# The end of an FFN kernel: the last quarter of the last tile as two pieces of 128 columns

## The chip, the cores and the metric

The kernel runs on one core of a Trainium2 chip. The metric is the device time of one execution in microseconds (us); lower is better. The kernel before was executed three times: 496.27, 496.76 and 497.31 us, median 496.76 us. One more execution was profiled; its own time and span stand in the table below.

## The reference

A grouped 1-D convolution with a conditioning term is followed by a dense layer with a low-rank correction, and all of it is added to the input. Cut to what matters:

```python
# x: (64, 64, 1024); 4 groups of 16 channels; 9 taps
y = conv1d(x, weight, groups=4) + (cond @ c_weight.T)[:, :, None] + fside[None, :, None]
base  = y @ kernel + bias                      # kernel: 1024 x 1024
A_eff = einsum('bn,nri->bri', gate, lora_A)    # 8 batches, rank 32
B_eff = einsum('bn,nor->bor', gate, lora_B)
delta = (y @ A_eff.T) @ B_eff.T + (y @ A_shared.T) @ B_shared.T
out = x + base + delta
```

## The kernel before

The 64 x 64 rows of x are worked in 8 batches (`b`) of 4 groups (`g`). A tile is one batch and one group: 128 rows of 1024 columns. There are 32 tiles in all, and the very last is `b = 7, g = 3`.

For a tile, TensorE runs the convolution, and then the dense product. Each operand of the dense product is split into a high and a low part of type fp32r (`y_hi`, `y_lo`, `w_hi`, `w_lo`), and three products are summed in PSUM: hi by hi, hi by lo, lo by hi. The contraction of 1024 is cut into `KC` = 8 chunks of 128 (`k`). So one column range of a tile is 8 x 3 = 24 matmuls, each with its own 128 x 128 stationary operand (a piece of `y`), and one more matmul (98 rows: low-rank part and bias, `b_cur` and `ax_st`) that closes the sum. All matmuls of the dense product that come before the end move 512 columns of `w` each (L921), and the matmul that closes them is L926. The low-rank product of `y` with A (L934) moves 256 columns past a 64-column stationary operand.

PSUM has two accumulators `main[0]` and `main[1]`, 1024 columns each, that is two banks of 512 each. Tiles alternate between them. VectorE (DVE) adds a finished tile to `res`, which holds x, and counts `main_free` up; the queue of SyncE (SP) waits for `main_free` and sends the tile out of `res`.

The last tile is not done like the others. Its parts, in order:

1. columns 0 to 511 in `main[1]`, 24 matmuls of 512 columns and L926;
2. the third quarter, columns 512 to 767, in the other bank of `main[1]`: `quarter(2, k)`, 24 matmuls of 256 columns (L909), and `quarter_rank(2)` (L912);
3. the last quarter, columns 768 to 1023, in `main[0]`, in the same form. Before it TensorE waits until DVE has emptied `main[0]` of the tile before.

Each of the parts counts `tile_done` up; DVE adds it (L789 for the first, L794 for the quarters), and SP stores it (L317):

```python
for n, part in enumerate((slice(0, 512), slice(512, 768), slice(768, 1024))):
    sp.wait_ge(main_free, NB * G + n)
    sp.dma_start(out_t[...], res[:, G - 1, part])
for g in range(G):
    sp.wait_ge(stored[g], 16 * (NB + 2 * (g == G - 1)))
```

The program ends when SP has seen every store's completion. Every engine's stream is in program order, written by hand; no scheduler moves anything. The functions that the change touches:

Of the kernel before, what the change touches and what calls it, by code (L numbers as in the profile page):

```python
# [7 lines left out]
ALU = mybir.AluOpType  # L8
# [3 lines left out]
P = 128  # L12
NS, C, L = 64, 64, 1024
D = 1024
G, CG, TAPS = 4, 16, 9
CD = 128
NL, R = 16, 32
NB = 8
# [5 lines left out]
KC = 8  # L24
R8, RQ = 8, R // 8
STACK = 3 * R
ROWS = STACK + 2
# [17 lines left out]


NP = MB // 2
FT = 6
SUM, EVEN, ODD = range(3)


def adaln_ffn(nc, x, x_rows, x_first, small, conv_w, kern, bias, lora_a, lora_b, shared, out):
# [9 lines left out]
    with ctx:  # L62
        def sb(name, shape, dt=F32):
            return ctx.enter_context(nc.sbuf_tensor(name, shape, dt))

        def ps(name, shape):
            return ctx.enter_context(nc.psum_tensor(name, shape, F32))

        def sem(name):
            return ctx.enter_context(nc.semaphore(name))  # L70

        def early(*specs):

            with ExitStack() as own:
                return [own.enter_context(nc.sbuf_tensor(*s)) for s in specs]
# [12 lines left out]
        res = sb("res", [P, G, D])  # L88
        la, = early(("la", [P, RQ, L], F32))
        be_hi, = early(("be_hi", [P, RQ, 512], F32R))  # L90
        xd_hi, xd_lo = sb("xd_hi", [P, 2, NP, SB], F32R), sb("xd_lo", [P, 2, NP, SB], F32R)
        ax_st, ax_sum = sb("ax_st", [P, 2 * P], F32R), sb("ax_sum", [R, 2 * P])
# [6 lines left out]
        x_tr = sb("x_tr", [P, MB + 1, SB, G])  # L99
        x_hi, x_lo = sb("x_hi", [P, 2, 2, NP + 1, SB], F32R), sb("x_lo", [P, 2, 2, NP + 1, SB], F32R)  # L100
        t_hi, t_lo = sb("t_hi", [P, G, WIN, CG], F32R), sb("t_lo", [P, G, WIN, CG], F32R)
# [5 lines left out]
        b_cur = sb("b_cur", [P, D], F32R)  # L107
        ctx_all = sb("ctx_all", [P, G, NS])
        ident, gmix = early(("ident", [P, P], F32), ("gmix", [P, NB, R8], F32))
        xd = sb("xd", [P, NP, SB])  # L110
        y_hi, y_lo = (y_hi0, y_hi1), (y_lo0, y_lo1)

        main = [ps(f"main{i}", [P, D]) for i in range(2)]
# [29 lines left out]
        tile_done, main_free = sem("tile_done"), sem("main_free")  # L143
        res_in = [sem(f"res_in{g}") for g in range(G)]
        stored = [sem(f"stored{g}") for g in range(G)]
# [12 lines left out]

        def x_raw(g, i0=0, i1=NP + 1):
            return x_tr[:, 2 * i0:2 * i1, :, g].rearrange("p (i e) n -> p e i n", e=2)  # L160

        def x_block(e, i0, g):
            return x_tr[:, 2 * i0 + e:2 * i0 + e + 2 * NP - 1:2, :, g]

        def x_half(half):
            return ((0, XSPLIT // 2), (XSPLIT // 2, NP + 1))[half]

# [12 lines left out]

            return b_cur[0:ROWS, :].rearrange("p (oh o8 ol) -> p o8 oh ol", oh=2, o8=R8)[:, 4 * n:4 * n + 4]

        def last_part(q):
            return (main[1][:, 512:768], main[0][:, 0:256])[q - 2]

        def small_part(i):
            return sm[:, SMALL[i]:SMALL[i + 1]]
# [4 lines left out]
        def f_bank(part):  # L192
            return (conv[0], conv[1], spare)[part][:, :]
# [18 lines left out]
        def _(sp):  # L212
# [99 lines left out]
            begin(NB - 1)  # L312
            turns(NB - 1, more_x=False, more_res=False)

            for n, part in enumerate((slice(0, 512), slice(512, 768), slice(768, 1024))):
                sp.wait_ge(main_free, NB * G + n)
                sp.dma_start(out_t[G - 1, (NB - 1) * SB:NB * SB, :, part], res[:, G - 1, part]).then_inc(stored[G - 1], 16)  # L317
            for g in range(G):
                sp.wait_ge(stored[g], 16 * (NB + 2 * (g == G - 1)))


        @block.gpsimd
# [119 lines left out]
        def _(act):  # L442
# [38 lines left out]
            def x_high(u, h, t):  # L481
# [6 lines left out]
                else:  # L488
                    act.wait_ge(conv_ready, u * FT + (3 * t - 7))
                act.wait_ge(xd_done, u * 4 + (2 * t - 7))  # L490
# [83 lines left out]
        def _(dve):  # L574
# [75 lines left out]
            def y_pair(b, h, t):  # L650
# [3 lines left out]
                term = ctx_all[:, 2 * h + t, bass.ds(b * SB, SB)].unsqueeze(1).broadcast_to([P, NP, SB])  # L654
                dve.wait_ge(conv_ready, u * FT + (at + 1))
                dve.wait_ge(y_turned, u * CT + 2 * t)
                nc.vector.tensor_tensor(y_add[:, 1, :].rearrange("p (m n) -> p m n", n=SB),  # L657
                                        f_bank(SUM).rearrange("p (m n) -> p m n", n=SB), term, ALU.add).then_inc(conv_free, 1)
                for e, part in enumerate((EVEN, ODD)):
                    dve.wait_ge(conv_ready, u * FT + (at + 2 + e))  # L660
                    dve.wait_ge(conv_free, u * FT + (at + 1 + e))
                    nc.vector.tensor_tensor(y_add[:, e, :], f_bank(part), y_add[:, 1, :], ALU.add).then_inc(conv_free, 1)
                for e in range(2):
                    dve.wait_ge(conv_free, u * FT + (at + 2 + e))
                    dve.wait_ge(ylo_done, u * CT + (2 * t + e - 5))
# [116 lines left out]
            with dve.Fori(1, NB - 1) as b:  # L782
# [5 lines left out]
            dve.wait_ge(tile_done, NB * G)  # L788
            nc.vector.tensor_tensor(res[:, G - 1, 0:512], main[1][:, 0:512], res[:, G - 1, 0:512],  # L789
                                    ALU.add).then_inc(main_free, 1)  # L790
            for q in (2, 3):
                part = slice(q * 256, (q + 1) * 256)
                dve.wait_ge(tile_done, NB * G + (q - 1))
                nc.vector.tensor_tensor(res[:, G - 1, part], last_part(q), res[:, G - 1, part], ALU.add).then_inc(main_free, 1)  # L794


        @block.tensor
        def _(pe):
            mm = nc.tensor.matmul
# [46 lines left out]
            def fast(b, h, t):  # L846
# [12 lines left out]
                for part in (SUM, EVEN, ODD):  # L859
                    if not (isinstance(u, int) and u == 2 and t == 0):  # L860
                        pe.wait_ge(conv_free, u * FT + (3 * t - 6 + part))
                    (t_h, t_l), (x_h, x_l) = taps[part], blocks[part]
# [39 lines left out]
                              lb[:, oh, s * 512:(s + 1) * 512], start=True, stop=True)  # L902
                last.then_inc(b_mm, 1)

            def quarter(q, k):

                yh, yl = y_hi[1][:, 1, k, :], y_lo[1][:, 1, k, :]
                for lhs, rhs, first in ((yh, w_hi, True), (yh, w_lo, False), (yl, w_hi, False)):
                    mm(last_part(q), lhs, rhs[:, k, q * 256:(q + 1) * 256], start=k == 0 and first, stop=False)  # L909

            def quarter_rank(q):
                mm(last_part(q), ax_st[0:ROWS, P:2 * P],  # L912
                   b_cur[0:ROWS, :].rearrange("p (oh o8 ol) -> p o8 oh ol", oh=2, o8=R8)[:, 2 * q:2 * q + 2],
                   start=False, stop=True).then_inc(tile_done, 1)

            def dense(h, t, k, halves=(0, 1), products=(0, 1, 2)):
                yh, yl = y_hi[h][:, t, k, :], y_lo[h][:, t, k, :]
                for i in products:
                    lhs, rhs, first = ((yh, w_hi, True), (yh, w_lo, False), (yl, w_hi, False))[i]
                    for n in halves:  # L920
                        mm(main[t][:, n * 512:(n + 1) * 512], lhs, rhs[:, k, n * 512:(n + 1) * 512],  # L921
                           start=k == 0 and first, stop=False)
# [86 lines left out]
            def unit(b, h, y=True, final=False, late=False):  # L1009
                u = b * 2 + h  # L1010
                nb, nh = (b, 1) if h == 0 else (b + 1, 0)
                pe.wait_ge(ylo_done, u * CT - 2)
                pe.wait_ge(main_free, u * 2 - 1)
                for k in range(4):
                    dense(h, 0, k)
                if y and not late:
                    fast(nb, nh, 0)
                for k in range(4, KC):
                    dense(h, 0, k)
                pe.wait_ge(ylo_done, u * CT)  # L1020
                pe.wait_ge(acur_done, b + 1)
                pe.wait_ge(ax_summed, u)
                with_a(h)
                pe.wait_ge(main_free, u * 2)

                def first_rank():
                    pe.wait_ge(axlo_done, u + 1)
                    if not (isinstance(b, int) and b == 0):
                        pe.wait_ge(b_loaded, b * 48)
                    lowrank(0)  # L1030

                if final:
                    for k in range(KC):
                        dense(h, 1, k, (0,))
                        if k == 4:
                            first_rank()
                    lowrank(1, (0,))
                    for k in range(KC):
                        quarter(2, k)
                    quarter_rank(2)  # L1040
                    pe.wait_ge(main_free, NB * G - 1)
                    for k in range(KC):
                        quarter(3, k)
                    quarter_rank(3)
                    return
                for k in range(3):
                    dense(h, 1, k)
                if not late:
                    first_rank()
                if y:  # L1050
                    fast(nb, nh, 0 if late else 1)
                if late:
                    first_rank()
                for k in range(3, 6):
                    dense(h, 1, k)
                if y and late:
                    fast(nb, nh, 1)
                for k in range(6, KC):
                    dense(h, 1, k)
                lowrank(1)  # L1060

            unit(0, 1, late=True)
            with pe.Fori(1, NB - 1) as b:
                unit(b, 0)
                unit(b, 1)
# [44 lines left out]
```

## Time and profile before

| what | value |
|---|---|
| median of 3 runs | 496.76 us |
| profiled execution, its own time | 497.13 us |
| profiled execution, span first to last instruction | 495.3 us |
| TensorE busy | 486.8 us, 98% of the span |
| VectorE busy | 319.3 us, 64% |
| GpSimd busy | 270.6 us, 55% |
| ScalarE busy | 166.9 us, 34% |
| granted TensorE clock, mean | 0.997 |

The profiled execution took 1.8 us more than its span, and 0.37 us more than the median of the runs. TensorE is busy in nearly every slice of the span; the last of the 40 slices of the page (12.4 us each) is the only late one in which it falls off, since the last add and the last store stand there alone.

### The profile page before, as it was taken

The page shows a single profiled execution, that of the slowest core. Times are in us where ns is not written, and L with a number is a line of the kernel's source. Part 1 is how long each engine was busy: PE and PEld are TensorE (multiplying, and loading weights), DVE is VectorE, ACT ScalarE, POOL GpSimd, SP SyncE. Part 2 cuts the span into 40 slices and gives each one's busy share as a digit, 9 for nine tenths or more (in the row PEclk, how much of TensorE's full clock was granted, in tenths as well). Part 3 has the DMA queues.
Part 4 walks back from the last instruction along what each step waited for, and adds up shares of the span by engine and source line. Part 5 has one row for each costly group of instructions (what it writes and reads, how often), then busy time and mean ns, then how long its engine had stood idle before and what let it go on. Part 6 is the DMA issues. An engine that isn't in the chain of part 4 may idle for free.

```text
span 495.3 us, 6738 instructions
## 1 busy us (share of the span) xinstructions
PE 486.8 (98%) x2417; PEld 403.1 (81%) x2417; DVE 319.3 (64%) x368; ACT 166.9 (34%) x205; POOL 270.6 (55%) x153
## 2 busy tenths in 40 slices
PE   6999999999999999999999999999999999999997
PEld 4785988888888888888888888888888888888886
DVE  4757575969667594948937595765939398473402
ACT  4575334333343152323324233431524224331100
POOL 0889865964837275661939247471846519392200
PEclk9899999999999999999999999999999999999999
DMA  8951858543624063431724245240734313241302
GB/s 252 422 233 60 255 122 226 221 134 108 218 53 125 40 232 107 106 95 29 248 72 119 71 152 183 50 129 26 249 90 113 88 36 84 63 123 66 96 32 85
DMA packets 16733, 64.56 MB, mean 130 GB/s; under 512 B 1520, under 2 KB 1968, under 8 KB 15824
## 3 DMA queue, kind: packets, MB, share of 16 engines
q1 hardware_dynamic: 16640, 64.35, 42.2%
q8 instruction: 8, 0.13, 0.1%
q10 hardware_dynamic: 80, 0.04, 0.0%
q14 instruction: 5, 0.04, 0.0%
HBM read 45.10 MB, written 18.87 MB: 129 GB/s over the span
## 4 chain that ended last, share of the span: by engine, by line
PE 97%; DMA 2%; DVE 0%; ACT 0%; SPq 0%; issue 0%
PE main L921 70%; PE rank L934 6%; PE main L926 3%; PE conv L839 3%; PE conv L863 3%; PE conv L864 3%; PE conv L865 3%; DMA x_tr<-in_x_first 2%; PE spare L865 1%; PE spare L864 1%; PE spare L863 1%; PE main L909 1%; PE main L888 1%; PE conv L901 1%; PE spare L876 0%; PE rank L876 0%
## 5 line engine op out<-in xcount | busy, mean ns | idle before, releaser
L921 PE MATMUL main<-w_hi,y_hi 128*128 128x512 f32 x504 | 155.6, 391 | 0.3 <-DVE a_eff L682 0.3
L921 PE MATMUL main<-w_lo,y_hi 128*128 128x512 f32 x504 | 155.1, 390 | 0.0
L921 PE MATMUL main<-w_hi,y_lo 128*128 128x512 f32 x504 | 154.7, 389 | 0.0
L376 POOL TENSOR_TENSOR y_lo<-y_stage,y_hi 128x512 fp32r<-128x512 f32 x56 | 93.2, 1686 | 34.3 <-ACT y_hi L479 34.3
L921 PEld LDWEIGHTS main<-w_lo,y_hi 128*128 128x128 f32 x504 | 94.5, 188 | 20.9 <-POOL w_lo L381 0.8
L921 PEld LDWEIGHTS main<-w_hi,y_lo 128*128 128x128 f32 x504 | 94.6, 188 | 19.9
L921 PEld LDWEIGHTS main<-w_hi,y_hi 128*128 128x128 f32 x504 | 93.4, 188 | 19.6 <-issue 0.7
L356 POOL TENSOR_TENSOR xd_lo<-xd,xd_hi 128x512 fp32r<-128x512 f32 x28 | 40.3, 1441 | 100.4 <-ACT xd_hi L491 100.3
L358 POOL TENSOR_TENSOR x_lo<-x_tr,x_hi 128x1024 fp32r<-128x1024 f32 x28 | 82.3, 2939 | 15.6 <-ACT x_hi L493 15.6
L493 ACT ACTIVATE x_hi<-x_tr 128x1024 fp32r<-128x1024 f32 x28 | 57.6, 2056 | 27.7 <-DVE x_tr L648 27.7
L479 ACT ACTIVATE y_hi<-y_stage 128x512 fp32r<-128x512 f32 x56 | 35.5, 634 | 91.9 <-DVE y_stage L666 91.9
L666 DVE STREAM_TRANSPOSE y_stage<-y_add 128x512 f32<-128x512 f32 x56 | 62.9, 1162 | 0.0
L738 DVE TENSOR_TENSOR ax_sum<-rank,ax_sum 32x256 f32<-32x256 f32 x16 | 6.6, 412 | 76.1 <-ACT ax_sum L504 76.1
L746 DVE TENSOR_TENSOR res<-main,res 128x1024 f32<-128x1024 f32 x31 | 37.5, 1210 | 22.9 <-PE main L926 22.9
L491 ACT ACTIVATE xd_hi<-xd 128x512 fp32r<-128x512 f32 x28 | 17.7, 633 | 90.9 <-DVE xd L644 90.9
L648 DVE TENSOR_TENSOR x_tr<-x_tr 128x512 f32<-128x512 f32 x28 | 44.7, 1597 | 1.0
L644 DVE TENSOR_TENSOR xd<-x_tr 128x512 f32<-128x512 f32 x28 | 40.0, 1428 | 1.2 <-POOL xd_lo L356 1.2
L657 DVE TENSOR_TENSOR y_add<-conv,ctx_all 128x512 f32<-128x512 f32 x28 | 19.2, 686 | 24.2 <-PE conv L865 24.2
L934 PE MATMUL rank<-y_hi,a_cur 128*64 128x256 f32 x128 | 29.9, 277 | 0.0
L934 PE MATMUL rank<-y_lo,a_cur 128*64 128x256 f32 x128 | 29.9, 277 | 0.0
L606 DVE STREAM_TRANSPOSE x_tr<-x_in 128x512 f32<-128x512 f32 (+2 forms) x48 | 29.4, 680 | 0.2
L504 ACT ACTIVATE ax_sum<-rank 32x256 f32<-32x256 f32 x16 | 6.0, 375 | 64.8 <-PE rank L934 64.8
(102 smaller groups left out, 503.3 us busy)
## 6 DMA issues: line engine op xcount, KB each, us to landing
res<-in_x SPq DMA_DIRECT2D x32, 512.0 KB
out<-res SPq DMA_DIRECT2D x31, 512.0 KB
x_in<-in_x_rows SPq DMA_DIRECT2D x6, 2048.0 KB, 12.5
w_raw<-in_L_ffn_kernel SPq DMA_DIRECT2D x4, 1024.0 KB, 16.8
b_cur<-b_scratch SPq DMA_DIRECT2D x21, 128.0 KB, 3.1
x_tr<-in_x_first SPq DMA_DIRECT2D x1, 2064.0 KB, 8.8
la<-in_L_ffn_lora_A SPq DMA_DIRECT2D x4, 512.0 KB, 10.1
lb<-in_L_ffn_lora_B SPq DMA_DIRECT2D x1, 2048.0 KB, 24.8
```

The source lines that it names most:

```text
L356: nc.gpsimd.tensor_tensor(xd_lo[:, t], xd[:, :, :], xd_hi[:, t].bitcast(F32), ALU.subtract).then_inc(xlo_done, 1)
L358: nc.gpsimd.tensor_tensor(x_lo[:, t, :, 0:NP], x_raw(2 * h + t, 0, NP), x_hi[:, t, :, 0:NP].bitcast(F32), ALU.subtract).then_inc(xlo_done, 1)
L376: nc.gpsimd.tensor_tensor(y_parity(y_lo, h, t, e), y_staged(e), y_parity(y_hi, h, t, e).bitcast(F32), ALU.subtract).then_inc(ylo_done, 1)
L479: nc.scalar.activation(y_parity(y_hi, h, t, e), y_staged(e), ACT.Copy).then_inc(yhi_done, 1)
L493: nc.scalar.activation(x_hi[:, t, :, 0:NP], x_raw(2 * h + t, 0, NP), ACT.Copy).then_inc(xhi_done, 1)
L606: nc.vector.transpose(x_tr[:, m0:m1, :, :].rearrange("p m n g -> p m (n g)"), blocks).then_inc(xt_done, 1)
L644: nc.vector.tensor_tensor(xd[:, :, :], x_block(0, 1, g), x_block(1, 0, g), ALU.subtract).then_inc(xd_done, 1)
L648: nc.vector.tensor_tensor(x_block(0, 0, g), x_block(0, 0, g), x_block(1, 0, g), ALU.subtract).then_inc(xd_done, 1)
L666: nc.vector.transpose(y_stage[:, e, :].rearrange("p (a l n c) -> p a n l c", a=2, l=2, n=SB), y_add[:, e, :].rearrange("p (a m n) -> p a n ...
L746: nc.vector.tensor_tensor(res[:, g, :], main[g % 2][:, :], res[:, g, :], ALU.add).then_inc(main_free, 1)
L921: mm(main[t][:, n * 512:(n + 1) * 512], lhs, rhs[:, k, n * 512:(n + 1) * 512], start=k == 0 and first, stop=False)
L934: last = mm(rank[0:2 * R, 0:2 * P], lhs, y[h][:, :, k, :], start=k == 0 and y is y_hi, stop=k == KC - 1 and y is y_lo)
```

## The change

The last quarter of the last tile becomes two pieces of 128 columns, 768 to 895 and 896 to 1023. Each has its own 24 matmuls and its own closing matmul, its own bank of `main[0]`, its own add and its own store. A list `LAST` holds the column bounds of the three pieces that follow the first half. The third quarter, columns 512 to 767, stays as it is.

```diff
+LAST = [512, 768, 896, 1024]
...
-        def last_part(q):
-            return (main[1][:, 512:768], main[0][:, 0:256])[q - 2]
+        def last_part(n):
+            return (main[1][:, 512:768], main[0][:, 0:128], main[0][:, 512:640])[n]
...
-            for n, part in enumerate((slice(0, 512), slice(512, 768), slice(768, 1024))):
+            for n, part in enumerate((slice(0, 512), *(slice(LAST[i], LAST[i + 1]) for i in range(3)))):
                 sp.wait_ge(main_free, NB * G + n)
                 sp.dma_start(out_t[G - 1, (NB - 1) * SB:NB * SB, :, part], res[:, G - 1, part]).then_inc(stored[G - 1], 16)
             for g in range(G):
-                sp.wait_ge(stored[g], 16 * (NB + 2 * (g == G - 1)))
+                sp.wait_ge(stored[g], 16 * (NB + 3 * (g == G - 1)))
...
-            for q in (2, 3):
-                part = slice(q * 256, (q + 1) * 256)
-                dve.wait_ge(tile_done, NB * G + (q - 1))
-                nc.vector.tensor_tensor(res[:, G - 1, part], last_part(q), res[:, G - 1, part], ALU.add).then_inc(main_free, 1)
+            for n in range(3):
+                part = slice(LAST[n], LAST[n + 1])
+                dve.wait_ge(tile_done, NB * G + (n + 1))
+                nc.vector.tensor_tensor(res[:, G - 1, part], last_part(n), res[:, G - 1, part], ALU.add).then_inc(main_free, 1)
...
-            def quarter(q, k):
+            def piece(n, k):
                 yh, yl = y_hi[1][:, 1, k, :], y_lo[1][:, 1, k, :]
                 for lhs, rhs, first in ((yh, w_hi, True), (yh, w_lo, False), (yl, w_hi, False)):
-                    mm(last_part(q), lhs, rhs[:, k, q * 256:(q + 1) * 256], start=k == 0 and first, stop=False)
+                    mm(last_part(n), lhs, rhs[:, k, LAST[n]:LAST[n + 1]], start=k == 0 and first, stop=False)
...
-                    for k in range(KC):
-                        quarter(2, k)
-                    quarter_rank(2)
-                    pe.wait_ge(main_free, NB * G - 1)
-                    for k in range(KC):
-                        quarter(3, k)
-                    quarter_rank(3)
+                    for n in range(3):
+                        if n == 1:
+                            pe.wait_ge(main_free, NB * G - 1)
+                        for k in range(KC):
+                            piece(n, k)
+                        piece_rank(n)
```

On TensorE, this is the end of the program before: the close of the third quarter (L912), then the last quarter's 24 matmuls of 256 columns and its close.

```order
640 L912 MATMUL main<-b_cur,ax_st 128x256
641 L909 MATMUL main<-w_hi,y_hi 128x256 [waits main_free]
642 L909 MATMUL main<-w_lo,y_hi 128x256
643 L909 MATMUL main<-w_hi,y_lo 128x256
...
665 L912 MATMUL main<-b_cur,ax_st 128x256
666 L62 UNCONDITIONAL_BRANCH
```

And this is the same place with the change (L911 and L914 are the old L909 and L912):

```order
640 L914 MATMUL main<-b_cur,ax_st 128x256
641 L911 MATMUL main<-w_hi,y_hi 128x128 [waits main_free]
642 L911 MATMUL main<-w_lo,y_hi 128x128
643 L911 MATMUL main<-w_hi,y_lo 128x128
...
665 L914 MATMUL main<-b_cur,ax_st 128x128
666 L911 MATMUL main<-w_hi,y_hi 128x128
667 L911 MATMUL main<-w_lo,y_hi 128x128
...
690 L914 MATMUL main<-b_cur,ax_st 128x128
691 L64 UNCONDITIONAL_BRANCH
```

Where 25 matmuls of 256 columns stood there are now 50 of 128 columns. Everything ahead of row 641 is as it was, and the one wait stands at the same place.

On VectorE, the end of the program before, from the add of tile `g = 2` (L746) on, through the three adds of the last tile:

```order
175 L738 TENSOR_TENSOR ax_sum<-rank,ax_sum 32x256 [waits ax_half]
176 L740 TENSOR_TENSOR ax_st<-ax_sum,ax_st 32x256 [waits axhi_done]
177 L746 TENSOR_TENSOR res<-main,res 128x1024 [waits res_in2,tile_done]
178 L789 TENSOR_TENSOR res<-main,res 128x512 [waits tile_done,res_in3]
179 L794 TENSOR_TENSOR res<-main,res 128x256 [waits tile_done] x2
180 L62 UNCONDITIONAL_BRANCH
```

With the change:

```order
176 L742 TENSOR_TENSOR ax_st<-ax_sum,ax_st 32x256 [waits axhi_done]
177 L748 TENSOR_TENSOR res<-main,res 128x1024 [waits res_in2,tile_done]
178 L791 TENSOR_TENSOR res<-main,res 128x512 [waits tile_done,res_in3]
179 L796 TENSOR_TENSOR res<-main,res 128x256 [waits tile_done]
180 L796 TENSOR_TENSOR res<-main,res 128x128 [waits tile_done] x2
181 L64 UNCONDITIONAL_BRANCH
```

The second add of 256 columns has become two of 128, each with a wait of its own on `tile_done`. SP's last store of 256 columns has become two of 128 in the same way.

## Rows read from the trace of the kernel before

**Rows 1.** The page: busy time of the engines, and the chain by engine.

```profile
PE 486.8 (98%) x2417; PEld 403.1 (81%) x2417; DVE 319.3 (64%) x368; ACT 166.9 (34%) x205; POOL 270.6 (55%) x153
...
PE 97%; DMA 2%; DVE 0%; ACT 0%; SPq 0%; issue 0%
```

**Rows 2.** The chain that ended last, its last pieces: start us, us, what.

```profile
488.75 2.88 PE main L909 x24
491.63 0.14 PE main L912
...
491.79 0.42 DVE res L794
```

**Rows 3.** Timeline of the end: start us, us, engine, line, operation, tiles, [idle before].

```profile
484.75 0.60 SPq L247 DMA_DIRECT2D out<-res  x1
...
488.47 0.28 PE L912 MATMUL main<-b_cur,ax_st 98*128 98x256 f32 x1
...
488.59 0.28 PE L909 MATMUL main<-w_hi,y_hi 128*128 128x256 f32 x1
...
491.35 0.19 PEld L912 LDWEIGHTS main<-b_cur,ax_st 98*128 98x128 f32 x1
491.47 0.28 PE L912 MATMUL main<-b_cur,ax_st 98*128 98x256 f32 x1
...
492.24 0.60 SPq L317 DMA_DIRECT2D out<-res  x1
```

**Rows 4.** Short stretches: PE, PEld, DVE, ACT, POOL busy, PEclk, DMA share, GB/s.

```profile
485.75:486.00 0.25, 0.25 (x5) 0.25 (x4) 0.14 (x1) 0.00 (x0) 0.00 (x0) 1.00 0.00 0
486.00:486.25 0.25, 0.25 (x4) 0.25 (x4) 0.25 (x1) 0.00 (x0) 0.00 (x0) 1.00 0.66 164
493.25:493.50 0.25, 0.00 (x0) 0.00 (x0) 0.00 (x0) 0.00 (x0) 0.00 (x0) 1.00 0.05 16
493.50:493.75 0.25, 0.00 (x0) 0.00 (x0) 0.00 (x0) 0.00 (x0) 0.00 (x0) 1.00 0.52 86
...
494.50:494.75 0.25, 0.00 (x0) 0.00 (x0) 0.00 (x0) 0.00 (x0) 0.00 (x0) 1.00 0.00 0
```

**Rows 5.** Timeline, two matmuls each of L934 and of L921.

```profile
477.94 0.28 PE L934 MATMUL rank<-y_lo,a_cur 128*64 128x256 f32 x1
...
479.30 0.28 PE L934 MATMUL rank<-y_lo,a_cur 128*64 128x256 f32 x1
...
481.93 0.39 PE L921 MATMUL main<-w_hi,y_lo 128*128 128x512 f32 x1
...
482.61 0.39 PE L921 MATMUL main<-w_hi,y_lo 128*128 128x512 f32 x1
```

**Rows 6.** Groups by shape: xcount | busy us, mean ns | idle before. PEld is the load.

```profile
L921 PEld LDWEIGHTS main<-w_hi,y_lo 128*128 128x128 f32 x504 | 94.6, 188 | 19.9
L934 PEld LDWEIGHTS rank<-y_hi,a_cur 128*64 128x64 f32 x128 | 17.2, 134 | 0.6
...
L814 PEld LDWEIGHTS main<-ident,z_all 64*128 64x128 f32 x16 | 1.1, 138 | 0.1
```

**Rows 7.** Timeline of the start, plain fp32 matmuls and loads (L804, L808, L814).

```profile
2.55 1.06 PE L804 MATMUL main<-ident 128*128 128x256 f32 x2
3.23 1.79 PEld L808 LDWEIGHTS rank<-sm,cw_rep 128*128 128x128 f32 x8 [0.34 <-issue]
...
5.17 1.07 PEld L814 LDWEIGHTS main<-ident,z_all 64*128 64x128 f32 x16
```

**Rows 8.** Lines L808 and L804: duration ns min/median/max.

```profile
L808 PEld LDWEIGHTS rank<-sm,cw_rep x8: 288/333/338, 3.2 to 4.7; 128*128 128x128 f32 x8
...
L804 PE MATMUL main<-ident x4: 634/634/796, 1.5 to 3.0; 128*128 128x256 f32 x4
```

**Rows 9.** Groups of VectorE by shape: the last tile's adds.

```profile
L794 DVE TENSOR_TENSOR res<-main,res 128x256 f32<-128x256 f32 x2 | 0.8, 424 | 4.8 <-PE main L912 4.8
L789 DVE TENSOR_TENSOR res<-main,res 128x512 f32<-128x512 f32 x1 | 0.7, 692 | 1.1 <-PE main L926 1.1
```

More of the change, by code:

```diff
@@ L903, in mix_b, with piece_rank @@
                 last.then_inc(b_mm, 1)
-            def quarter(q, k):
+            def piece(n, k):
                 yh, yl = y_hi[1][:, 1, k, :], y_lo[1][:, 1, k, :]
                 for lhs, rhs, first in ((yh, w_hi, True), (yh, w_lo, False), (yl, w_hi, False)):
-                    mm(last_part(q), lhs, rhs[:, k, q * 256:(q + 1) * 256], start=k == 0 and first, stop=False)
-            def quarter_rank(q):
-                mm(last_part(q), ax_st[0:ROWS, P:2 * P],
-                   b_cur[0:ROWS, :].rearrange("p (oh o8 ol) -> p o8 oh ol", oh=2, o8=R8)[:, 2 * q:2 * q + 2],
+                    mm(last_part(n), lhs, rhs[:, k, LAST[n]:LAST[n + 1]], start=k == 0 and first, stop=False)
+            def piece_rank(n):
+                mm(last_part(n), ax_st[0:ROWS, P:2 * P],
+                   b_cur[0:ROWS, :].rearrange("p (oh o8 ol) -> p o8 oh ol", oh=2, o8=R8)[:, LAST[n] // 128:LAST[n + 1] // 128],
                    start=False, stop=True).then_inc(tile_done, 1)
```

## The prediction

> **What bounds the kernel now.** I read the page first. TensorE is busy for 98% of the span and holds 97% of the chain that ended last [rows 1]. So whatever makes TensorE's stream longer makes the kernel longer, one for one, unless the time is given back at the very end, where TensorE has already stopped.
>
> That end is what the change touches, so next I read the end of the chain of waits and the timeline beside it. The reader should see three things. First, the last quarter's 24 matmuls take 2.88 us, back to back, and after the closing matmul come only one add of 0.42 us and the store [rows 2]. Second, TensorE doesn't wait at the border between the quarters: the third quarter's last matmul starts at 488.47 and the last quarter's first at 488.59, which is the ordinary distance [rows 3]. Third, from the start of the last add (491.79) to the end of the span (495.3) there are 3.5 us in which TensorE does nothing, and only this stretch can be shortened by smaller pieces.
>
> Of the 3.5 us, 0.42 are the add, and 0.03 pass until SP issues the store at 492.24 [rows 2, 3]. The DMA share has sunk to 0.05 (the last of the earlier stores) and jumps to 0.52 at 493.50, 1.26 us after the issue; these data move for about 1.0 us, to 494.50, and 0.8 us more pass to the end [rows 4]. Is the 1.26 us a queue behind earlier stores? The store issued at 484.75 found the DMA engines idle, and its data began to move in the stretch from 486.00, 1.25 us later [rows 3, 4]. The same delay with nothing ahead, so nothing is held up by a queue, and an earlier store for half of the data frees nothing. What scales with the size of the last piece is then the add and part of the 1.0 us of data.
>
> **What the change gives back.** The add: 692 ns for 512 columns, 424 ns for 256 [rows 9], so 268 ns per 256 columns and a fixed part of about 156 ns. For 128 columns that makes 290 ns, a gain of 0.13 us. The data: the last store still has 128 rows, now of 512 bytes instead of 1 KB. If only the number of rows counted, nothing is gained; if only bytes, half of 1.0 us. I take 0.15, since the row count stays and the engines' start is staggered; the bounds are 0 and 0.5. The issue on SP (0.60 us) and the two fixed delays stay. Together I take 0.28 us back, with bounds 0.13 and 0.63.
>
> The extra add and the extra store of columns 768 to 895 are free: their cover is the second piece's TensorE work, 1.6 us at the very least (below), against an add of 0.29 us and an issue of 0.60 us. Were that cover gone, SP's issue would be late by at most 0.6 us. The bank change costs nothing: the wait for `main_free` stands where it did, and both banks of `main[0]` were freed by the same add, which is over when TensorE arrives.
>
> **What it costs TensorE.** 25 matmuls of 256 columns become 50 of 128. The count of columns is the same; the number of stationary operands to be loaded doubles. Everything turns on the distance from one 128-column matmul to the next, call it g. The trace has no fp32r matmul narrower than 256 columns, so g is bounded from both sides.
>
> *Below.* If only streaming counted: 512 columns go at 0.68 / 3 = 0.227 us a matmul [rows 5], 256 at 2.88 / 24 = 0.120 (488.59 to 491.47, rows 3). The difference is 0.107 us for 256 columns, so 128 would go at 0.066.
>
> *The load.* The closing matmul's load starts at 491.35, one distance ahead of its matmul at 491.47 [rows 3], which is when the matmul before it starts. So each load has the time of one matmul, and I take it that it has to be through the array's input before the next can be. Its recorded duration is 188 ns for 128 columns and 134 ns for 64 [rows 6]: 54 ns for 64 columns, thus 108 ns for 128 columns on top of a fixed 80 ns of latency. At 256 moving columns (107 ns of streaming) such a load just fits; at 128 (54 ns) it doesn't. What a matmul stream does when the load is the longer part is seen at the start of the program, with plain fp32: two matmuls of 256 columns (L804) stand (1.06 - 0.634) = 0.43 us apart [rows 7, 8], while at L808 only 64 columns move, a quarter, and the 8 loads still stand (1.79 - 0.333) / 7 = 0.208 us apart [rows 7, 8], not 0.11. The load sets a floor there, and I expect one here. With the floor g is between 0.107 (the load alone) and 0.120 (today's distance, if what is above 0.107 there is paid at each change of the operand: with a 64-column operand the same 256 columns go at 1.36 / 12 = 0.113 [rows 5], so part of it is tied to the operand). I take 0.115.
>
> The row that speaks against a floor is L814: 16 loads of 128 columns at (1.07 - 0.138) / 15 = 0.062 us [rows 6, 7]. But those loads are recorded at 138 ns, 50 ns shorter than ours, and they have 64 rows. Read on a line through the two pairs of duration and distance (138 and 62, 333 and 208), a load of 188 ns comes every 0.100 us. That is near the floor of 0.107, and far from 0.066.
>
> The Trainium skill (TensorE: Matmul & The Clock Gate, section LDWEIGHTS) gives the load as columns divided by 1.2, that is 107 ns for 128 columns, which the difference of the two durations above bears out. The same page, section Back-to-back issue gap, states 81 ns per matmul of 128 columns in a sustained stream of loads and matmuls; it would speak for a gap below the load's own time. By 81 ns the sum below would be +0.8 us instead of +2.4. No row here shows such a stream in fp32r.
>
> **The sum.** The last quarter's first matmul starts at 488.59. Now 49 distances follow until the very last one starts, where it was 24 (2.88 us). That last one lasts 0.23 instead of 0.28 (0.39 less 0.28 makes 0.11 for 256 columns [rows 3, 5]), and the add starts about 0.04 us behind it as before: 0.32 us becomes 0.27.
> - TensorE: 49 x 0.115 = 5.64, plus 0.27, less 2.88 and 0.32: +2.71 us. With 0.107 it is +2.31, with 0.120 it is +2.95.
> - Add: -0.13. Last store: -0.15.
> - Net +2.4 us on the profiled execution's 497.13, which makes 499.5. That execution stood 0.37 above the median of the runs, so for the median I predict 496.76 + 2.4 = 499.2 us, +0.5%.
>
> The clock is full in all of these stretches [rows 4], and TensorE has no new idle time ahead of its last matmul, so I add nothing for it.
>
> **The rivals.**
> *A. The stream is the bound, the loads hide (not slower).* g = 0.066: 49 x 0.066 + 0.27 - 3.20 = +0.30, less 0.28 given back: 0.0, 496.8 us. With the whole 0.63 given back it is -0.3, 496.4. For it: the 0.062 us of L814, and that loads are seen to overlap in their recorded durations. Against it: L808, and 188 against 138 ns. It decides from g below 0.092 on (then the net is under 1.0 us, 0.2%).
> *B. Loads partly hidden.* A load may begin before the one ahead is wholly in; half way between 0.066 and 0.107, g = 0.087: +1.3 - 0.28 = +1.0, 497.8 us. The page's 81 ns is a case of this.
> *C. A narrow fp32r matmul falls back to the pace of plain fp32.* The plain L804 takes 0.43 us for 256 columns, where fp32r takes 0.120; at that pace 128 columns take 0.21, up to 0.227 if it is as long as a 512-column fp32r matmul. Then 49 x 0.213 = 10.4, +0.4 for a longer last one, - 3.2: +7.7, less 0.28: +7.4, about 504.2; with 0.227 504.9. For it: all of the kernel's fp32r matmuls have 256 or 512 moving columns, so the trace can't exclude that narrow ones go another way. Against it: nothing in it shows a switch between the two paces either, and the load of fp32r (188 ns) is recorded unlike the plain one (333 ns).
> *D. The last store's data take longer as 512-byte rows.* At worst it stays at 1.0 us or grows by 0.2; it moves every case by that and changes none.
>
> **How the numbers follow.** Load floor 0.60, rival C 0.23, rival B 0.07, rival A 0.10. The likeliest case has its own range of 498.4 to 500.0 (g from 0.107 to 0.120, 0.13 to 0.63 given back, and 0.2 for the runs' scatter). C is likelier than A and B together, so the range for 8 in 10 reaches up to it: 498.3 to 505.2. It leaves out A, B and a little of the rest. A measurement of this kernel tells about 0.2%, or 1.0 us, from no change. A gives "same", with a small part faster; half of B gives "same"; all else is slower: faster 0.02, same 0.12, slower 0.86.
>
> **What would show it.** In the profile after, L911 with 128x128 has its starts 0.107 to 0.120 us apart and loads still recorded near 188 ns: step one right. The last two pieces take 5.6 us or so, the last add 0.29 us, and the add of the first 128 columns lies under TensorE's work. Starts 0.066 apart mean A, near 0.21 mean C. If the last store's data move for half the time, the gain at the end is 0.5 and not 0.15. The prediction is wrong if g isn't near the load's time, or if the time after the last matmul changes by more than 0.7 us.

## The result, and the profile after

| | before | after |
|---|---|---|
| median, 7 runs each | 496.76 us | 499.14 us |
| all runs | 495.75 to 497.42 | 497.85 to 500.98 |
| ratio to before | | 1.0046, interval 1.003 to 1.0061 |
| profiled execution, span | 495.3 us | 496.9 us |
| TensorE busy | 486.8 us | 490.1 us |

The changed kernel is slower by 0.46% (0.3 to 0.6%), that is by 2.3 us (1.5 to 3.0). Predicted were 499.2 us and +2.4 us.

First the page of the changed kernel, busy time by engine, against [rows 1]:

```profile
PE 490.1 (99%) x2442; PEld 406.3 (82%) x2442; DVE 319.4 (64%) x369; ACT 167.0 (34%) x205; POOL 270.6 (54%) x153
```

TensorE has 25 more matmuls and 3.3 us more busy time; no other engine has moved. Next the end of the chain of waits of the changed kernel (start us, us, what), against [rows 2]:

```profile
488.29 0.12 PE main L914
488.41 2.63 PE main L911 x24
491.04 0.11 PE main L914
491.15 2.68 PE main L911 x24
493.83 0.13 PE main L914
493.96 0.02 issue
493.98 0.29 DVE res L796
```

Where 24 matmuls of 256 columns took 2.88 us, there are now two groups of 24 matmuls of 128 columns, and each of them takes 2.63 to 2.68 us. Half the columns per matmul saved 0.2 us per group, and there are two groups. 2.68 / 24 = 0.112 us from one matmul to the next, against 0.120 with twice the columns.

Now the timeline of the changed kernel at the border between third quarter and first narrow piece, and at the end, against [rows 3]:

```profile
488.13 0.28 PE L914 MATMUL main<-b_cur,ax_st 98*128 98x256 f32 x1
488.13 0.19 PEld L911 LDWEIGHTS main<-w_hi,y_hi 128*128 128x128 f32 x1
488.25 0.23 PE L911 MATMUL main<-w_hi,y_hi 128*128 128x128 f32 x1
488.25 0.19 PEld L911 LDWEIGHTS main<-w_lo,y_hi 128*128 128x128 f32 x1
488.31 0.28 PE L911 MATMUL main<-w_lo,y_hi 128*128 128x128 f32 x1
488.36 0.19 PEld L911 LDWEIGHTS main<-w_hi,y_lo 128*128 128x128 f32 x1
...
493.67 0.28 PE L914 MATMUL main<-b_cur,ax_st 98*128 98x128 f32 x1
493.98 0.29 DVE L796 TENSOR_TENSOR res<-main,res 128x128 f32<-128x128 f32 x1 [2.50 <-PE main L914]
494.30 0.60 SPq L319 DMA_DIRECT2D out<-res  x1
```

The first distance is 0.06 us (488.25 to 488.31), since that load had been made under the 256-column matmul before it. From then on the loads follow each other every 0.11 us (488.25, 488.36), and the matmuls go at the loads' pace. The last add is 0.29 us long where it was 0.42.

Last, the stretches in which the last store's data move in the changed kernel (columns as in [rows 4]):

```profile
493.50:495.50 2.00, 0.45 (x4) 0.30 (x3) 0.29 (x1) 0.00 (x0) 0.00 (x0) 1.00 0.00 0
495.50:495.75 0.25, 0.00 (x0) 0.00 (x0) 0.00 (x0) 0.00 (x0) 0.00 (x0) 1.00 0.39 84
495.75:496.00 0.25, 0.00 (x0) 0.00 (x0) 0.00 (x0) 0.00 (x0) 0.00 (x0) 1.00 0.54 162
496.00:496.25 0.25, 0.00 (x0) 0.00 (x0) 0.00 (x0) 0.00 (x0) 0.00 (x0) 1.00 0.07 16
```

They begin 1.2 us after the issue, as before, and move for 0.5 to 0.6 us instead of 1.0.

The two profiled executions are best compared from the last quarter's first matmul on, because what lies ahead of it is the same program and yet differs by 0.3 us between the two executions (488.59 and 488.25). That difference arises at the start: from the first matmul of L934 (L936 in the changed kernel), at 55.8 and 55.4 us, to its last, at 479.3 and 479.0, both take 423.5 us. From the last quarter's first matmul to the end of the span it was 6.7 us and is now 8.7.

### The profile page after: what moved, and what is told of

It reads as the page before. It is cut to its first block, busy times and chain, and to the rows that moved or that the text cites. A ratio compares the mean times of both kernels' runs of the same rounds, so it can differ in the third digit from the quotient of the medians.

```text
span 496.9 us, 6790 instructions
## 1 busy us (share of the span) xinstructions
PE 490.1 (99%) x2442; PEld 406.3 (82%) x2442; DVE 319.4 (64%) x369; ACT 167.0 (34%) x205; POOL 270.6 (54%) x153
## 4 chain that ended last, share of the span: by engine, by line
PE 97%; DMA 2%; ACT 0%; DVE 0%; SPq 0%; issue 0%
PE main L923 69%; PE rank L936 6%; PE main L928 3%; PE conv L841 3%; PE conv L865 3%; PE conv L866 3%; PE conv L867 3%; DMA x_tr<-in_x_first 2%; PE main L911 2%; PE spare L867 1%; PE spare L866 1%; PE spare L865 1%; PE main L890 1%; PE conv L903 1%; PE spare L878 0%; PE rank L878 0%
## 5 line engine op out<-in xcount | busy, mean ns | idle before, releaser
L936 PE MATMUL rank<-y_hi,a_cur 128*64 128x256 f32 x128 | 29.9, 277 | 0.0
L936 PE MATMUL rank<-y_lo,a_cur 128*64 128x256 f32 x128 | 29.9, 277 | 0.0
```

Of the source, the lines that this page charges most:

```text
L936: last = mm(rank[0:2 * R, 0:2 * P], lhs, y[h][:, :, k, :], start=k == 0 and y is y_hi, stop=k == KC - 1 and y is y_lo)
```

## Experiments

Nine of the ten kernels below were timed against the kernel before in several rounds; its median was 496.6 to 497.5 us in these. Ratios are to it. Where two ratios can't be told apart, the profile's rows decide.

**1. Half the stationary operand.** In the two narrow pieces only:

```diff
-                yh, yl = y_hi[1][:, 1, k, :], y_lo[1][:, 1, k, :]
+                w = P if n == 0 else 64
+                yh, yl = y_hi[1][:, 1, k, 0:w], y_lo[1][:, 1, k, 0:w]
```

and `last_part(n)[0:w]`, `ax_st[0:ROWS, P:P + w]` to match.

> The changed kernel, with the 50 matmuls of 128 columns given a stationary operand of 64 columns instead of 128 (rows 64 to 127 of the last 256 output columns are left unfinished). My theory: the distance of 0.112 us between 128-column matmuls is the load of 128 stationary columns. A load of 64 should need half, 0.054 to 0.056 us, and streaming 128 columns 0.054 plus some ns, so the distance falls to about 0.060 us and the kernel is 49 x 0.052 = 2.5 us shorter than the changed one: about 496.6 us, level with before. Rival: a narrow fp32r matmul has a floor of its own near 0.11 us, whatever is stationary; then the distance stays at 0.11 us and the time at 499.1 us.

Measured: 496.4 us, ratio 0.9984 (0.9971 to 0.9997). From the chain of waits of this kernel:

```profile
488.35 1.44 PE main L912 x24
489.79 0.06 PE main L916
489.85 1.44 PE main L912 x24
```

1.44 / 24 = 0.060 us. The matmuls move the same 128 columns as in the changed kernel; only the stationary operand is half, and the distance fell by 0.052. The rival, a floor of narrow fp32r matmuls themselves, falls.

**2. A quarter of the stationary operand.** As above with `w = 32`.

> The changed kernel with a stationary operand of 32 columns in the two last pieces (rows 32 to 127 of the last 256 output columns are left unfinished). With 128 stationary columns the distance between 128-column matmuls was 0.112 us, with 64 it was 0.060. Load floor: with 32 the load takes 0.027 and is hidden under the 0.053 of streaming; what stands above the streaming halves with the stationary columns (13 ns at 128, 7 at 64 behind 256 moving columns), so the distance is 0.056 to 0.058 us and hardly falls any more. Rival: the distance follows the stationary columns all the way, 0.030 to 0.035 us.

Measured: 496.0 us in one run. The chain:

```profile
488.06 1.44 PE main L912 x24
```

Again 0.060 us, not 0.030. With 32 stationary columns the load is hidden and streaming is the bound. The direction was right; the size was not: I expected the 7 ns above pure streaming to halve, and they stayed (0.060 less 0.053, which is half of the 0.107 us that 256 columns stream for).

**3. Four pieces of 64 columns.** Banks in turn, each piece with its own add and store:

```diff
-LAST = [512, 768, 896, 1024]
+LAST = [512, 768, 832, 896, 960, 1024]
...
+                        if n > 2:
+                            pe.wait_ge(main_free, NB * G + n - 1)
```

> The last quarter in four pieces of 64 columns (100 matmuls), banks in turn, each with its add and store. My theory (load floor): the distance stays at 0.112 us though the columns are halved again; TensorE needs 99 x 0.112 = 11.1 us for the last quarter, 5.6 more than the changed kernel, the last add is about 0.07 shorter and the last store 0.1 to 0.2; in all +5.4 over the changed kernel, about 504.5 us (+1.6% over before). Rival (the distance still depends on the columns, 0.112 being partly streaming): 0.112 - 0.027 = 0.085 us a matmul, 99 x 0.085 = 8.4 us, about 501.9 us.

Measured: 509.82 us, ratio 1.0252 (1.0233 to 1.027), 5 us above what either theory gave. The chain of waits of this kernel:

```profile
487.44 2.60 PE main L911 x24
490.04 0.11 PE main L914
490.15 4.82 PE main L911 x24
494.97 0.21 PE main L914
495.18 5.12 PE main L911 x24
```

The first piece is what the load floor says: 2.60 / 24, about 0.11 us, though it moves only 64 columns. In the second piece the distance nearly doubles, and in the third it is 5.12 / 24 = 0.213. The stretches of the same kernel show why (the seventh number is the granted clock):

```profile
487.44:489.94 2.50, 2.50 (x25) 2.50 (x24) 0.42 (x1) 0.00 (x0) 0.00 (x0) 1.00 0.53 188
489.94:490.44 0.50, 0.50 (x6) 0.50 (x5) 0.22 (x1) 0.00 (x0) 0.00 (x0) 0.92 0.46 170
490.44:492.44 2.00, 2.00 (x12) 2.00 (x11) 0.00 (x0) 0.00 (x0) 0.00 (x0) 0.50 0.21 64
```

The granted clock went from 1.00 (2.4 GHz) to 0.50 (1.2 GHz) some 2.9 us into the 64-column matmuls, and TensorE was recorded busy all the time. All four executions show it: 508.75 to 510.31 us, with a mean granted clock of 0.982 to 0.984. So the load floor's own part is right in the first piece, and the excess is the clock: 0.213 less 0.112 makes 0.10 us for each of some 71 matmuls, 7 us. In this execution it is 21.2 us from the last quarter's first matmul (487.27) to the end of the span (508.5), 14.5 more than before; less the 7 that is 7.5, where the load floor had 7.8 (5.4 over the changed kernel). The medians differ by less, 12.8 us. Part of that is the start: here the last quarter began 1.3 us earlier than in the profiled execution before, and from 12 to 15 us the granted clock is 1.00, where it was 0.50 in that execution.

**4. The same four pieces with half the stationary operand.** Kernel 3 with `w = 64` as in kernel 1.

> The kernel with four pieces of 64 columns, with a stationary operand of 64 columns instead of 128 in them (rows 64 to 127 of the last quarter are left unfinished). There the granted clock fell to 1.2 GHz 2.9 us into the narrow matmuls, which moved 64 columns per 0.112 us. Load floor: a load of 64 columns takes half, so the distance is 0.054 to 0.060 us, the last quarter 99 x 0.057 = 5.6 us, about what the two 128-column pieces of the changed kernel take, and columns move at the same pace as there. If the clock follows how many columns move per time, it stays at 2.4 GHz and the time is about 499.1 us. Rival: it follows something else (matmuls of 64 columns as such, or how much of the array is in use); then it falls again in this stretch, the distance goes to about 0.11 us, and the time is 501 to 502 us.

Measured: 499.22 us, ratio 1.0038 (1.0017 to 1.0059). The chain, and one stretch over its 100 narrow matmuls:

```profile
489.39 1.38 PE main L912 x24
490.76 0.06 PE main L916
490.82 1.40 PE main L912 x24
```

```profile
489.20:495.00 5.80, 5.80 (x102) 5.80 (x100) 1.10 (x4) 0.00 (x0) 0.00 (x0) 1.00 0.38 126
```

0.058 us a matmul, and the granted clock stayed at 1.00 over the whole 5.8 us. So 64-column matmuls as such don't bring the clock down, nor does a stationary operand that fills half of the array. This answers two explanations; one pair of kernels doesn't show what the rule is.

**5. The change made twice.** The third quarter too in two pieces of 128 columns:

```diff
-LAST = [512, 768, 896, 1024]
+LAST = [512, 640, 768, 896, 1024]
```

> The change made twice: the third quarter too in two pieces of 128 columns, so 100 matmuls of 128 columns instead of 50, each piece with its bank, add and store. The run with 64-column pieces showed that TensorE's granted clock fell from 2.4 to 1.2 GHz in the middle of the narrow matmuls, with TensorE busy, and their distance went from 0.112 to 0.213 us. If only the load floor counts here, the third quarter grows as the last did, 2.88 to 5.4 us: +2.5 us over the changed kernel, about 501.7 us, ratio 1.0095. Rival (the clock falls under 128-column matmuls too, given a longer stretch of them): part of the 11 us stands at 0.213 us a matmul and the time is up to 5 us longer, 504 to 507 us.

Measured: 501.63 us, ratio 1.0095 (1.0079 to 1.0111): the first theory's number. Its chain:

```profile
485.69 2.63 PE main L911 x24
488.32 0.11 PE main L914
488.43 2.68 PE main L911 x24
...
494.02 2.68 PE main L911 x24
```

Every piece takes 2.63 to 2.68 us, the last as the first, so the clock didn't fall in 11 us of 128-column matmuls. The price of the change is a price per load, and it adds up.

**6. The gain at the end alone, on one queue.** TensorE as before the change; the last quarter's add and store in two halves:

```diff
+                for i in range(2):
+                    part = slice(768 + i * 128, 896 + i * 128)
+                    nc.vector.tensor_tensor(res[:, G - 1, part], last_part(q)[:, i * 128:(i + 1) * 128], res[:, G - 1, part],
+                                            ALU.add).then_inc(main_free, 1)
```

> TensorE as before the change (25 matmuls of 256 columns); only the last quarter's add and store are made in two halves of 128 columns, both on VectorE and SyncE's queue. This is the gain at the end without TensorE's price. The two adds take 0.29 + 0.29 instead of 0.42 us (+0.16). The last store's data and landing shrink by 0.47 as in the changed kernel. If SyncE issues one store per 0.60 us and the second waits for that, it is issued 0.93 us after the first add's start instead of 0.45 (+0.48) and the net is 0.0: 496.8 us. If the issue doesn't hold the second back, -0.3: 496.5 us.

Measured: 497.26 us, ratio 1.001 (0.9998 to 1.0021), no gain. The timeline of this kernel:

```profile
491.46 0.28 PE L918 MATMUL main<-b_cur,ax_st 98*128 98x256 f32 x1
491.79 0.49 DVE L799 TENSOR_TENSOR res<-main,res 128x128 f32<-128x128 f32 x2 [2.57 <-PE main L918]
492.11 1.24 SPq L317 DMA_DIRECT2D out<-res  x2
```

The two adds overlap and take only 0.49 us together, but the second store is issued when the first's 0.60 us are over, at 492.75 (492.11 and 1.24, less 0.60), half a microsecond later than the single store of before (492.24). The gain of the smaller store pays for that and no more.

**7. The same on two queues.** The first half's store is issued by ScalarE:

```diff
+            act.wait_ge(main_free, NB * G + 2)
+            act.dma_start(out_t[G - 1, (NB - 1) * SB:NB * SB, :, 768:896], res[:, G - 1, 768:896]).then_inc(stored[G - 1], 16)
```

> TensorE as before the change; the last quarter's add and store in two halves of 128 columns as in the run with the split add, but the first half's store is issued by ScalarE's queue, so SyncE's is free for the second. There the second store waited for the first's 0.60 us issue (issued 0.96 us after the first add's start). Here it should be issued at about 0.21 + 0.28 + 0.04 = 0.53 us after it, against 0.45 before the change, and land 0.47 sooner: -0.4 us against before, ratio 0.999. Rival: the two stores share the DMA engines at the end, so the last one lands no sooner than 2.6 us after its issue: +0.1 us, ratio 1.000.

Measured: 497.26 us, ratio 1.0008 (0.9996 to 1.0021). That is the rival's number; 0.999 lies outside the interval. Timeline and one stretch:

```profile
491.91 1.20 ACTq L572 DMA_DIRECT2D out<-res  x1
492.11 0.60 SPq L317 DMA_DIRECT2D out<-res  x1
```

```profile
493.25:494.25 1.00, 0.00 (x0) 0.00 (x0) 0.00 (x0) 0.00 (x0) 0.00 (x0) 0.76 0.47 131
```

The second store is issued at 492.11, 0.5 us after the first add's start at 491.59, as hoped, but now both halves' data move in the same 1.0 us, like the one store before. In these runs a smaller last store lands sooner only if its sibling is out of the way: in kernel 6 the second store ends 2.7 us after its issue (492.75 to 495.4), here 2.9 (492.11 to 495.0), and before the change it was 3.1. That the two share the DMA engines is the likely reason; the rows don't separate their packets. From the last matmul's start to the end it is 3.77 us against 3.86: 0.1 us won, too little to measure.

**8. Smaller pieces in computing, one store.** The changed kernel with its two pieces sent in one store of 256 columns.

> The changed kernel with its two last pieces worked and added apart but sent in one store of 256 columns at the end. TensorE as in the changed kernel. If the smaller last store is what gave 0.47 us back, that is lost: +0.47 over the changed kernel, about 499.6 us, and in the profile the last store needs 2.6 us from issue to landing as before, not 2.1. If 512-byte rows against 1 KB rows make no difference the time stays at 499.1 us.

Measured: 498.78 us, ratio 1.0037 (1.0024 to 1.005). By time it can't be told from the changed kernel; what was expected, +0.1%, is below the interval's width. The waits of SP tell it, first of the changed kernel, then of this one (waited for: us in total, times, longest us):

```profile
SPq L321 <- DMA out<-res: 1.4, 1, 1.4
```

```profile
SPq L321 <- DMA out<-res: 1.9, 1, 1.9
```

With the single store the wait is 1.9 us, as it was before the change; with half the size it is 1.4. So the smaller store is what gave back 0.5 us.

**9. Both pieces in one bank.** This undoes "a bank of its own". TensorE must then wait for the first piece's add:

```diff
-            return (main[1][:, 512:768], main[0][:, 0:128], main[0][:, 512:640])[n]
+            return (main[1][:, 512:768], main[0][:, 0:128], main[0][:, 128:256])[n]
...
+                        if n == 2:
+                            pe.wait_ge(main_free, NB * G + 2)
```

> The changed kernel with both 128-column pieces in the same bank of main[0] (columns 0 to 127 and 128 to 255), for which TensorE must wait with the second piece until the first has been added. It undoes the part 'each in a bank of its own'. In the profile of the changed kernel the first piece's add runs from 491.19 to 491.48, and TensorE's next matmul starts at 490.99; if it has to wait it starts at about 491.55, so +0.55 us over the changed kernel, about 499.7 us. Rival: the wait is hidden, since TensorE loads the next operand meanwhile and drains; then 499.1 us.

Measured: 499.74 us, ratio 1.006 (1.0044 to 1.0076). Its timeline between the pieces:

```profile
491.27 0.28 PE L914 MATMUL main<-b_cur,ax_st 98*128 98x128 f32 x1
491.59 0.29 DVE L796 TENSOR_TENSOR res<-main,res 128x128 f32<-128x128 f32 x1 [2.32 <-PE main L914]
...
491.93 0.19 PEld L911 LDWEIGHTS main<-w_hi,y_hi 128*128 128x128 f32 x1 [0.53 <-DVE res L796]
491.94 0.33 PE L911 MATMUL main<-w_hi,y_hi 128*128 128x128 f32 x1 [0.39 <-DVE res L796]
```

The distance at the border is 0.67 us (491.27 to 491.94) instead of 0.11. Even the load waited, so nothing hides the add. The separate banks are worth about 0.6 us within the change; against the kernel before they win nothing, since it has no second piece that could wait.

**10. The opposite direction.** The whole second half in 25 matmuls of 512 columns, then adds and stores of 256, 128 and 128 columns, the middle store on ScalarE's queue.

> The opposite direction: the last tile's whole second half in 25 matmuls of 512 columns (no quarters), then three adds of 256, 128 and 128 columns and three stores, the middle one on ScalarE's queue. TensorE: 24 x 0.227 instead of 49 x 0.120 from the first to the last matmul's start, -0.43, its last matmul 0.11 longer: -0.32 us. After it the adds take 0.34 + 0.21 + 0.28 = 0.8 instead of 0.42 (+0.4), the last store lands 0.47 sooner, but may wait for SyncE, whose issue of the 256-column store ends at about +1.0: +0.1. Net -0.3 us against before, ratio 0.9994. Rival: narrower pieces at the end are worth more than TensorE's 0.3 us, and it is slower than before by 0.3.

Measured: 497.78 us, ratio 1.0019 (1.0005 to 1.0032), slower: the rival. Its timeline:

```profile
492.10 0.39 PE L927 MATMUL main<-b_cur,ax_st 98*128 98x512 f32 x1
492.52 0.82 DVE L795 TENSOR_TENSOR res<-main,res 128x256 f32<-128x256 f32 x3 [4.92 <-PE main L927]
492.98 1.24 SPq L317 DMA_DIRECT2D out<-res  x2
493.18 1.24 ACTq L572 DMA_DIRECT2D out<-res  x1
```

The matmuls save their 0.4 us, but from the last matmul's start to the end of the span it is 4.8 us (492.10 to 496.9) instead of 3.9. All 512 columns are left to be stored after TensorE has stopped, and the last store is issued only at 493.62. From there to the end it is 3.2 us, no less than the 3.1 of the single store before, so the 0.47 us that the smaller store was to give back didn't come.

No kernel that does the whole work beats the one before. Its quarters of 256 columns sit where load and streaming are about equal.

## Why the prediction was right

*The load sets the distance (right).* The distance g from one 128-column matmul to the next was predicted between 0.107 and 0.120 with 0.115 taken, and measured 0.112. The reason was tested and not only the number: with half the stationary columns the distance fell to 0.060 (kernel 1), with half the moving columns it stayed at about 0.11 (kernel 3, first piece), and the price doubles with the number of loads (kernel 5). The loads' own distances show it: 128 stationary columns every 0.112 us, 64 every 0.058 (kernel 4). The load row of before, 188 ns against 134, gave 108 ns for 128 columns; 0.112 - 0.058 = 54 ns for 64 columns is the same slope. Rival A falls. The counter row L814 doesn't fall with it: its loads of 128 columns and 64 rows do stand 0.062 us apart. They are also operands of transposes in plain fp32. No run took these differences apart, so why these loads come faster stays open.

*The rows of the program's start (misread).* The prediction looked at the granted clock at the end [rows 4], but not at the start, where rows 7 and 8 stand. Kernel 3 shows what a load of 128 columns looks like at a granted clock of 0.50:

```profile
490.66 0.33 PEld L911 LDWEIGHTS main<-w_hi,y_lo 128*128 128x128 f32 x1
```

It takes 0.33 us instead of 0.19, and the loads come every 0.213 us. The plain fp32 loads of L808 have the same numbers (333 ns, 0.21 us apart). So L808, and L804 right ahead of it, very likely ran at half the clock. The clock column reads 1.00 there, but it counts time without a clock record as full, and the first record of that trace stands at 5.16 us. L814 starts at 5.17 and is the first row at the full clock. In the changed kernel the first record comes at 8.40 us, and the same 16 loads (now L816) take longer, 0.104 us apart on average:

```profile
5.23 1.78 PEld L816 LDWEIGHTS main<-ident,z_all 64*128 64x128 f32 x16 [0.20 <-DVE z_all L595]
```

They take these 1.78 us, against 1.07, in every trace but that of the kernel before. Three things follow. L808 is still a row for a load floor, since L804 moves four times its columns in only twice the time at the same clock; but its 0.208 us is a price at half the clock. The line through L814 and L808 joins rows at two clocks, and that its 0.100 us came near 0.107 was luck. And rival C's pace, 0.43 us for 256 columns, was a pace at the lower clock, where 0.213 us is what fp32r reaches too: its chance of 0.23 and the upper part of the range, up to 505.2 us, had no ground. What carried the prediction is the pair of load durations 188 and 134 ns, both from rows at the full clock.

*TensorE's sum (nearly right).* Predicted +2.71 us. Measured 5.42 (488.25 to 493.67) plus 0.31 to the add, less 3.20: +2.53. The distance was a little smaller, the first one only 0.06, and the matmul's recorded length stayed at 0.28 where I took 0.23.

*The add (right).* 0.29 us, -0.13 as predicted.

*The last store (mis-sized).* I took 0.15 from bounds of 0 and 0.5; measured are 0.47 (from the add's end to the span's end 3.116 us before, 2.642 after). The data time went by bytes and hardly by the number of rows; kernel 8 shows that it is the store's size. Here the prediction reasoned from an unchanged row count, and that was the weaker bound.

The sum by these parts is 2.53 - 0.13 - 0.47 = +1.9 us for the profiled execution, where the prediction had +2.4 and the runs' medians differ by 2.4, with an interval of 1.5 to 3.0. Both errors went the same way, and the agreement of the median to 0.1 us is partly luck.

*Rival A* (stream-bound) and *rival C* (0.21 us at the full clock) didn't occur. Kernel 3 did reach 0.213 us, but at half the clock. *Rival B*, loads partly hidden, fell too: the Trainium skill (TensorE: Matmul & The Clock Gate, section Back-to-back issue gap) gives 81 ns for 128 columns, and these fp32r matmuls with full operands took 112. The Trainium skill's rule for the load on that page (section LDWEIGHTS), columns divided by 1.2, makes 107 ns. The measured slope agrees at the full clock (54 ns for 64 columns); at a granted clock of 0.50 it doesn't, the loads of 128 columns came every 213 ns there. *Rival D* was the wrong way round. Extra add and extra store were hidden, as stated: DVE and SP waited for TensorE before each piece. Two small slips of the prediction's sums change nothing: the limit for rival A is a distance of 0.086 us with 0.28 given back (0.092 needs nearly the whole 0.63), and rival C's times come out 0.1 us lower than written.

## What to carry to other kernels

Count the loads, not the columns: where every matmul brings a new stationary operand, cutting the moving operand below the point at which streaming takes as long as the load (256 columns against a full fp32r operand here) makes each cut cost nearly a whole load per matmul, 25 x 0.112 = 2.8 us per cut (+2.5 measured). What a finer last piece can give back comes from the last add and the last store's data time, here 0.6 us of 3.5, and it should be set against that price first. And before a row from the start of a program is used as a price, compare it with the same instruction in another execution: the clock may not be the same. Splitting the add and the store without splitting the matmuls is free for TensorE, but the queue's issue time (kernel 6) or, as is likely, the shared DMA engines (kernel 7) took the gain here.

## What the runs showed of the hardware that I had not expected

- The granted clock fell from 1.00 to 0.50 while TensorE was recorded busy without a gap, in a run of 64-column matmuls 0.11 us apart behind full stationary operands (kernel 3). It stayed at 1.00 in 5.8 us of 64-column matmuls 0.058 us apart (kernel 4) and in 11 us of 128-column matmuls 0.112 us apart (kernel 5). The Trainium skill (TensorE: Matmul & The Clock Gate, Part 1: The HAM clock gate) tells of the half rate as the default and as what follows idle stretches; this one came in a stretch that the records call busy. What decides it isn't settled here.
- Two adds in a row on VectorE without a wait between them overlapped: 0.49 us for both, at 0.28 and 0.29 us each (kernel 6).
- A store issued by ScalarE's queue took 1.20 us to issue (kernel 7) and 1.24 (kernel 10), against 0.60 on SyncE's.
- At 128 moving columns the distance is 0.060 us with 64 and with 32 stationary columns (kernels 1 and 2): about 7 ns above streaming stay, though the load is half or a quarter as long.
